# A hybrid layer on one core: attention pipelined over halves of the queries, packed diagonal maxima, sums by shuffle, and a projection spread over the last half and the FFN

## The reference

```python
x = x + attn_a(layernorm(x))   # 16 heads of 16, rotary embedding, causal softmax, projection Wo
x = x + ffn(layernorm(x))      # silu(x @ Wg) * (x @ Wu) @ Wd, hidden 768, int weights / 127
x = x + attn_b(layernorm(x))   # RWKV-like: token shift, low-rank mixes, decayed scan, group norm, gate, Wo
x = x + ffn(layernorm(x))      # the same FFN
```

```python
scores = einsum('bhtd,bhsd->bhts', q, k) / 4
scores = where(causal, -inf, scores)
out = einsum('bhts,bhsd->bhtd', softmax(scores), v)   # then out @ Wo.T
```

## Time and profile before

| | |
|---|---|
| median of 3 runs | 3501.13 us (3500.01 to 3502.6) |
| the profiled execution | 3503.35 us, its span 3501.6 |
| PE busy | 3000.5 us, 86% of the span |
| DVE busy | 2487.5 us, 71% |
| ACT busy | 1311.2 us, 37% |
| POOL busy | 1307.0 us, 37% |
| mean granted TensorE clock | 0.939 |

### The profile page before, as it was taken

One profiled execution on the slowest core, in us unless ns is written; L12 is line 12 of the kernel. 1 busy time (PEld: TensorE's weight loads), 2 busy tenths in 40 slices (PEclk: granted clock), 3 DMA queues, 4 the chain that ended last, 5 costly groups with the idle time before them and its releaser, 6 DMA issues.

```text
span 3501.6 us, 47094 instructions
## 1 busy us (share of the span) xinstructions
PE 3000.5 (86%) x17056; PEld 1850.4 (53%) x17056; DVE 2487.5 (71%) x5137; ACT 1311.2 (37%) x2721; POOL 1307.0 (37%) x1244
## 2 busy tenths in 40 slices
PE   2488989889889888889888898898988889898898
PEld 1236565365743567345763457635565355653667
DVE  4675787667775677856878568775687757876565
ACT  0264223622336322453225531265313643236322
POOL 0023551235512454124631347213462235522455
PEclk9699999999999999899998999899998999999999
DMA  3600032000510006000150002400023000330000
GB/s 130 110 2 13 19 64 54 2 13 19 79 39 13 2 19 98 20 14 10 29 97 2 14 10 46 80 2 13 19 46 71 2 13 19 52 66 2 1 1 13
DMA packets 68885, 115.01 MB, mean 33 GB/s; under 512 B 10795, under 2 KB 64075, under 8 KB 65531
## 3 DMA queue, kind: packets, MB, share of 16 engines
q1 hardware_dynamic: 68627, 111.51, 16.2%
HBM read 74.69 MB, written 33.65 MB: 31 GB/s over the span
## 4 chain that ended last, share of the span: by engine, by line
PE 46%; DVE 32%; POOL 9%; issue 5%; ACT 4%; DMA 2%; SPq 0%; DVEq 0%; ACTq 0%; POOLq 0%
DVE mxp L967 9%; PE PB L1311 7%; PE PB L1296 5%; PE PB L1386 5%; PE PB L1371 5%; PE PB L1282 4%; DVE arena L1156 4%; PE PB L1425 3%; PE PB L1344 3%; DVE arena L1165 2%; PE PB L1460 2%; DVE attn L890 2%; ACT arena L722 2%; PE PB L1450 2%; DVE stats L879 1%
## 5 line engine op out<-in xcount | busy, mean ns | idle before, releaser
L967 DVE TENSOR_REDUCE mxp<-PB 128x1 f32<-128x512 f32 (+3 forms) x1536 | 752.9, 549 | 160.8 <-PE PB L1282 87.1
L722 ACT ACTIVATE arena<-PB 128x512 f32<-128x512 f32 (+3 forms) x1536 | 650.5, 508 | 455.5 <-PE PB L1296 450.6
L1282 PE MATMUL PB<-arena 96*128 96x512 bf16 (+3 forms) x1536 | 513.0, 362 | 106.7 <-DVE mxp L967 64.3
L582 POOL TENSOR_SCALAR_AFFINE_SELECT arena<-arena 128x512 f32<-128x512 f32 x256 | 163.5, 639 | 1003.7 <-ACT arena L722 1003.3
L1296 PE MATMUL PB<-arena 99*128 99x512 bf16 (+3 forms) x1536 | 467.7, 344 | 26.5 <-DMA arena<-augT 19.3
L1282 PEld LDWEIGHTS PB<-arena 96*128 96x128 bf16 x1536 | 154.8, 102 | 428.0 <-DVE mxp L967 326.1
L1311 PE MATMUL PB<-arena 128*32 128x512 f32 (+3 forms) x3072 | 339.9, 515 | 15.5 <-ACT attn L711 13.7
L1371 PE MATMUL PB<-xh,wgu 128*128 128x512 f32 x768 | 313.7, 408 | 42.3 <-DVE xl L1034 29.0
L592 POOL TENSOR_TENSOR hl<-arena,hh 128x512 fp32r<-128x512 f32 x192 | 248.3, 1293 | 262.3 <-ACT hh L747 256.9
L1371 PE MATMUL PB<-xl,wgu 128*128 128x512 f32 x768 | 309.6, 403 | 2.8 <-issue 2.8
L1555 PE MATMUL PB<-arena 128*128 128x128 f32 x1792 | 235.4, 283 | 56.1 <-DVE arena L1156 46.7
(11 more groups left out here) (139 smaller groups left out, 5372.6 us busy)
## 6 DMA issues: line engine op xcount, KB each, us to landing
arena<-parts SPq DMA_DIRECT2D x112, 256.0 KB, 9.7
parts<-arena SPq DMA_DIRECT2D x192, 128.0 KB
arena<-parts SPq DMA_DIRECT2D x16, 768.0 KB, 18.4
arena<-in_x SPq DMA_DIRECT2D x16, 512.0 KB, 4.5
arena<-parts SPq DMA_DIRECT2D x16, 512.0 KB, 21.0
xres<-in_x SPq DMA_DIRECT2D x16, 512.0 KB, 4.8
out<-xres SPq DMA_DIRECT2D x16, 512.0 KB, 3.4
wgu<-arena SPq DMA_DIRECT2D x2, 768.0 KB, 4.5
```

The costliest lines, as they stand in the source:

```text
L582: pool.affine_select(out=a, in_=a, compare_op=ALU.is_ge, fill=0.0, base=0, pattern=[[0, HG], [1, 128]], channel_multiplier=-1).then_inc(ma ...
L722: act.activation(pt[:, U % 3, h, 0:n], bank(b, "score", t)[:, 0:n], ACT.Exp, scale=DH ** -0.5).then_inc(act_emptied, 1)
L967: dve.reduce_max(mxp[:, g % 2, h, col:col + 1], bank(b, "max", g * NPC + k)[:, 0:n], axis=AX.X).then_inc(dve_emptied, 1)
L1282: last = mm(ps[:, 0:n], qst[0:AUG, h, 128 * i:128 * i + 128], kst[0:AUG, h, s0:s0 + n], start=True, stop=not diag)
```

## The change

Attention is now planned in blocks of a group and a half of its queries (k = 2g + f, eight blocks).

- Units come half by half: four for half 0, then eight for half 1. Blocks of maxima alternate between 11 items (half 0) and 27 (half 1); `score_steps` works out how many scores each step has: none before 15 steps (LAG) after block 0's last maximum, then at most 0.6 a step, and 1.27 a step from 15 steps after block 1. After the last maximum each step has one unit of four scores.
- Maxima over 256 keys are packed two heads to a bank and one reduce, those over 128 keys four heads to a bank and one reduce; 152 items a sequence instead of 192.
- The join of the maxima stays on VectorE; the split into three parts moves to GpSimd (`max_parts`), per half and with five instructions. One DMA per half carries the three rows.
- ScalarE copies a half out when that half is done. `den` is a stream shuffle that puts the sum's row on all 32 partitions of a head, and a reciprocal over all 512 columns; `over_sums` follows per half.
- The projection items 0 and 1 stand after the scores of unit 44 of 48, items 2 and 3 after the first gate and up items of the FFN, with the residual and LayerNorm of half 1 inside the FFN. The transposes of half 1 move from the third to the fifth step of the first FFN.
- The first FFN uses the space of queries and keys (`ffn_sets`), the next sequence's x0 and the split buffers have other places, queries and keys are laid out half by half.

The core of the diff:

```diff
 def score_units():
-    return [(j, f) for j in range(NT) for f in (0, 1) if 128 * j < HALF * (f + 1)]
+    return [(j, f) for f in (0, 1) for j in range(4 * f + 4)]
 def max_pieces():
     out = []
-    for i in range(NT):
-        out.append((i, 0, min(HALF, 128 * (i + 1)), i))
-        if i >= 4:
-            out.append((i, HALF, 128 * (i + 1) - HALF, NT + i - 4))
+    for f in (0, 1):
+        if f:
+            out.append([((h,), i, 0, HALF, i) for i in range(4, NT) for h in range(HG)])
+        else:
+            out.append([])
+        for a in (3, 2, 1, 0):
+            n = 128 * (a + 1)
+            heads = [(h,) for h in range(HG)] if a >= 2 else [(0, 1), (2, 3)] if a else [tuple(range(HG))]
+            out[f] += [(hs, 4 * f + a, HALF * f, n, 4 * f + a + 4 * f) for hs in heads]
     return out
...
+def score_steps():
+    done, credit, out = 0, 0.0, []
+    for t in range(NMAX):
+        ready = [k for k in range(2 * NG - 1) if t >= BLOCK_END[k] + LAG]
+        most = HG * (LAST_UNIT[ready[-1]] + 1) if ready else 0
+        credit = min(credit + (1.27 if t >= BLOCK_END[1] + LAG else 0.6), 2.0)
+        n = max(0, min(int(credit), most - done))
+        credit -= n
+        done += n
+        out.append(done)
+    while done < NSC:
+        done = min(NSC, HG * (done // HG + 1))
+        out.append(done)
+    return out
...
+AUG_STEP = [min(BLOCK_END[k] + AUG_AT, NMAX + 1) for k in range(2 * NG)]
+UNIT_STEP = [step_of(HG * U + HG - 1) for U in range(NG * len(UNITS))]
+OUT_AFTER = [LAST_UNIT[k] + (3 if k < 2 * NG - 2 else 2) for k in range(2 * NG)]
+DEN_STEP = [UNIT_STEP[OUT_AFTER[k]] + 4 for k in range(2 * NG - 2)]
+O_STEP = UNIT_STEP[NG * len(UNITS) - 4]
...
+                    for t in range(STEPS):
+                        if t in BLOCK_END:
+                            max_parts(BLOCK_END.index(t))
+                        for U in DIAG_UNITS:
+                            if UNIT_STEP[U] == t:
+                                mask_unit(U)
+                        if t in DEN_STEP:
+                            over_sums(DEN_STEP.index(t))
+                        if t == O_STEP:
+                            over_sums(2 * NG - 2)
                     ln_scale(1, b, 0)
-                    ln_scale(1, b, 1)
+                    over_sums(2 * NG - 1)
...
+                    def den(k):
+                        g, f = k // 2, k % 2
+                        sums = sumT[:, f, :].rearrange("p (i t) -> p i t", i=4)
+                        dve.wait_ge(pv_copied, 8 * b + k + 1)
+                        if b or k >= 2:
+                            dve.wait_ge(attn_normed, 8 * b + k - 1)
+                        dve.stream_shuffle(sums, attn[:, 4 * f:4 * f + 4, g, :], [DH] * 32).then_inc(den_chain, 1)
+                        dve.wait_ge(den_chain, 16 * b + 2 * k + 1)
+                        dve.reciprocal(sums, sums).then_inc(den_chain, 1)
...
+                    den(2 * NG - 2)
...
+                    dve.wait_ge(x_loaded[0], 16 * (b + 1))
+                    residual("o", 0, 0)
+                    residual("o", 1, 0)
+                    ln_half(1, 0)
+                    den(2 * NG - 1)
+                    x_low(1, 0, (0, 1))
...
+                        if t == O_STEP:
+                            out_proj(0)
+                            out_proj(1)
+                    pv(NG * len(UNITS) - 2)
+                    pv(NG * len(UNITS) - 1)
+                    transpose_x(1, (0, 1))
...
+                            if e == 1 and k == 1:
+                                out_proj(2)
+                                out_proj(3)
```

The three parts of `max_parts`, five instructions in a chain:

```diff
+                        pool.tensor_scalar(parts_[0], m, -1.0, 1.0, ALU.mult, ALU.mult).then_inc(aug_chain, 1)
+                        pool.tensor_tensor(augf[:, :, :], m, parts_[0], ALU.add).then_inc(aug_chain, 1)
+                        pool.tensor_scalar(parts_[1], augf[:, :, :], -1.0, 1.0, ALU.mult, ALU.mult).then_inc(aug_chain, 1)
+                        pool.tensor_tensor(augf[:, :, :], augf[:, :, :], parts_[1], ALU.add).then_inc(aug_chain, 1)
+                        pool.tensor_scalar(parts_[2], augf[:, :, :], -1.0, 1.0, ALU.mult, ALU.mult).then_inc(aug_chain, 1)
```

More of the change, by code:

```diff
@@ L106, in ahead @@
                 add(nxt, kind, ns, who)
-        for t in range(NSC + DELAY):
-            if t < NSC:
+        for t in range(STEPS):
+            if t < NMAX:
                 add(b, "max", (t,), "dve")
@@ L112, in psum_plan @@
                 add(b, "v", (2 + V_AT.index(t),), "act")
[L113 to L117, removed]
+            if t in AUG_STEP:
+                add(b, "aug", (AUG_STEP.index(t),), "dve")
+            add(b, "score", scores_of(t), "act")
+            if t == O_STEP:
+                add(b, "o", (0, 1), "dve")
         add(b, "ln1", (0, 1), "dve")
-        add(b, "o", (3,), "dve")
         ffn(b, 1)
@@ L487, in split_tile @@
         def split_tile(e, s):
-            return halves(spl[e // 4][:, e % len(parts_out[e // 4]), s, :])
+            return halves(spl[e // 4][e % len(parts_out[e // 4])][:, s, :])
         def halves(a):
@@ L596, in _ @@
                         h_low_part(1, 0, e)
-                        if e == 1 and ahead:
+                        if e == 0:
+                            ln_scale(1, b, 1)
+                        if e == 5 and ahead:
                             ln_scale(0, b + 1, 0)
@@ L1070, in ffn @@
                             gate(k, s, e)
-                            if e == 4 and k == 1 and ahead:
+                            if e == 6 and k == 1 and ahead:
                                 x0_norm(b + 1, 0)
@@ L1313, in pv, with out_proj @@
                         last.then_inc(pv_units, 1)
-                    for t in range(NSC + DELAY):
-                        if t in (0, 2 * NPC):
-                            pe.wait_ge(stacked[t // (2 * NPC)], 9 * 16 * (b + 1))
-                        if t < NSC:
-                            max_item(t // NPC, t % NPC)
+                    def out_proj(n):
+                        wait_bank(pe, b, "o", n)
+                        pe.wait_ge(attn_normed, 8 * b + 2 * NG - 1 + n // 2)
+                        for a in (0, 1):
+                            for g in range(NG):
+                                last = mm(bank(b, "o", n)[:, D * a:D * a + D], attn[:, 2 * n + a, g, :], wo[:, g, :],
+                                          start=(g == 0), stop=(g == NG - 1))
+                        last.then_inc(filled, 1)
```

355 lines of the change are left out of this document (168 added, 187 removed).

## The result

The changed kernel takes 3659.58 us (median of 4 runs, 3642.74 to 3666.68) against 3501.86 for the kernel before in the same comparison (3500.01 to 3503.1): a ratio of 1.0445, 95% interval 1.0428 to 1.0462. It is 158 us slower, where 3488 was forecast and 3565 was the end of the range. The profiled execution took 3642.74 us, its span 3640.9, the fastest of the four; five of the sequences behind the first take 440.1 to 440.7 us of it.

The account below looks back on a forecast made before the run. VectorE and TensorE, blocking each other through the six-bank ring, were taken as the bound. 33.5+86+33+6+56.6=215.1 us against 216.9, 1.8 less a sequence, 14.4 over eight, off 3503.35, gave 3488 us; range 3400 to 3565.

Parts of the forecast that it names:

- The reciprocal: Denominators on VectorE: 512 columns taken at 3.0 us, ends 0.68 and 4.5; with the shuffle 3.7 us a half.
- the floor of the aggregates: Reciprocal estimate: 6-element aggregates start 0.07 us apart; taken off the 16-element reciprocal's 0.14, this gives 2.5 us for 512.
- Rival (a): Denominators: reciprocal cheap at 0.68 us, TensorE becomes the bound, 10.3 us a sequence less, 3406 us; chance 0.20.
- (b): Denominators: reciprocal costs 4.4 us, the floor hidden; 9.5 us a sequence more, 3564 us; chance 0.17.
- I take 90%: Steps 52 to 151: VectorE's busy share rises from 82% to 90%; ends 95% (81 us) and 82% (96 us).
- The third stretch: Steps 52 to 151, maxima and scores together: VectorE's 79.5 us over 0.90, less 2, gives 86 us.
- the stops of 2.5 us: Steps 52 to 151: TensorE and ScalarE stop some 2.5 us behind each 3.7 us denominator piece on VectorE.
- rival (c): Steps 12 to 51 and ahead of the FFN: TensorE at half clock, 5 us a sequence net, 3528 us; chance 0.13.
- Until the last product: Scores alone 23.5 us, half the projection 7.2, its wait for GpSimd 2.3: 33 us.
- Until the FFN: From last product to FFN: copy, shuffle, reciprocal, two x_low and waits on VectorE, 6 us against 18.5 before.
- steps 0 to 51: Ramp, VectorE-bound: 32.5 us of maxima, join, copies and V items plus 1 us for half clock, 33.5 us.
- Packing and the split: Maxima on VectorE: packing saves 2.5 to 6 us a sequence, 4 taken; moving the split to GpSimd saves 4.

Follow-up runs that it names:

- e5: e3 with the four denominator steps of halves 0 to 4 put behind four successive maxima, no piece over 0.7 us; 3456.61 us, ratio 0.9887.
- e1: The changed kernel with the 512-column reciprocal of halves 0 to 4 cut into four of 128 columns behind successive maxima; 3570.09 us, ratio 1.0204.
- e11: The changed kernel with the reciprocal over 256 of the 512 columns, that part of the softmax left out; 3555.38 us, ratio 1.0157.
- e6: e5 with all four projection items back behind the last value product, residual and LayerNorm of both halves ahead of the FFN; 3359.21 us, ratio 0.9606.
- e7: e3 with the split of the maxima, five small instructions per half, moved from GpSimd back to VectorE; 3554.82 us, ratio 1.0166.
- e10: e5 with GpSimd's scaling of half 6 put ahead of the mask of unit 44 instead of behind it; 3413.52 us, ratio 0.9753.
- e8: e3 with banks still packed but one reduce per head, 40 more instructions a sequence; 3521.3 us, ratio 1.0073.
- e9: e6 with the changed kernel's denominators, a shuffle and one reciprocal of 512 columns; 3536.24 us, ratio 1.0108.
- e3: The changed kernel with the denominators of before (transpose, reciprocal of 16, copy, transpose) per half in one piece of 2.0 us; 3484.57 us, ratio 0.9956.

## Why the prediction was wrong

**The reciprocal.** Taken at 3.0 us with ends 0.68 and 4.5, it is 3.353. By form, in e5, e1 and e11:

```profile
L1065 DVE RECIPROCAL recip<-sumT 128x16 f32<-128x16 f32 x64 | 15.3, 240 | 0.8
```

```profile
L1060 DVE RECIPROCAL sumT<-sumT 128x128 f32<-128x128 f32 x256 | 230.6, 924 | 0.8
```

```profile
L1056 DVE RECIPROCAL sumT<-sumT 128x256 f32<-128x256 f32 x64 | 112.2, 1753 | 2.2
```

From 256 to 512 columns it is 1.600 us, 6.25 ns a column, on 0.15 us. By this slope the 0.14 us between two starts at 16 columns were 0.10 for the columns and 0.04 for the rest: the floor of the aggregates, 0.07, was the wrong one to take off. By the prediction's own slope (6.8 us a sequence for each us) this is 2.4 us, 19 us in all: it turns 3488 into 3507 and no more. Rival (a) is refuted and (b) had the right sign with too high a price of the instruction (4.4) and too low a price of each us.

**The step that failed: "I take 90%".** The third stretch was reckoned as VectorE's work over a share, 79.5/0.90, less 2. The work was right. The share was 79%, under the lower end of 82% and near the 80% that the prediction named as a sign of being wrong, since I took the stops of 2.5 us (five, 12.5 us; measured 13.75) as something that VectorE's busy time already pays for. It doesn't, because TensorE is the second bound: its modelled busy time is 78.2 us of the 80.8 in e6. A stretch in which two engines need 79 and 78 us has no room for 14 us in which only one of them works, and none to make up time at half clock. I had priced the clock in the ramp and at the FFN (rival (c), 5 us a sequence, where its own terms give 4), where the row that I had read showed it, and not behind the stops that I forecast myself.

TensorE's busy and idle time of steps 52 to 151 show what stood in its place:

| us | length | TensorE busy | TensorE idle | VectorE busy | clock |
|---|---|---|---|---|---|
| e5 | 80.0 | 77.4 | 2.6 | 69.2 | 1.00 |
| e1 | 92.5 | 84.1 | 8.4 | 78.3 | 0.93 |
| after | 100.9 | 86.6 | 14.3 | 79.3 | 0.88 |

From e5 to the changed kernel the stretch grows by 20.9 us: 11.7 are idle time of TensorE, 9.2 are longer busy time for the same matmuls, since TensorE spent 22 us of it at 0.50. Of the 20.9 us, 8.4 are due to the length of the piece (e1 to after). The other 12.5 stand in e1 too, where the same work comes in short pieces: VectorE's share was 85% there and 86% in e7, so 90% was too high for this much work however it is cut. Adding the five stops to TensorE's need (78+13.75, 92 us) would have come nearer than the share, but misses what the clock takes, and it doesn't explain e1.

**Until the last product.** Forecast 33, measured 35.4: the base of 23.5 us (its terms add up to 23.1; e6: 23.9) and the projection's 7.2 (e10: 7.17) were right, the wait for GpSimd was 3.58 instead of 2.3, and the projection took 8.64 instead of 7.2 behind it. **Until the FFN** 7.6 instead of 6: the reciprocal's 0.35, and 1.6 us in which the last shuffle stood behind the normalization of half 0 (1635.23 above), which the prediction had as done by then; **FFN** 56.3, forecast 56.6; **steps 0 to 51** 34.7, forecast 33.5.

**Packing and the split.** The packing is worth about what was said (e8), and a chain of the split costs VectorE 1.1 us where 1 was taken (e7).

**What I read as a gain of 12.5 us behind the last product** (18.5 to 6) was to be paid back by 9.5 in the scores and 8.7 in the FFN in my own sum, so spreading the projection was forecast as a loss of 5.7 us a sequence, 46 in all. It cost 97 us in all beside fast denominators (e6 against e5) and 118 to 123 beside slow ones (e9 against the changed kernel). The mechanism was in the text, at less than half its size.

Of e1's 12.5 us over e5, 5.8 are idle and 6.7 busy time of TensorE. How much of the idle time the lower clock brought on itself was not measured: no run held the clock while TensorE waited. What makes the clock fall behind one stop and not behind another stays open too.

## What to carry to other kernels

Where two engines both fill a stretch and meet in a ring of buffers, don't divide the work of one by a share that looks reachable. Add the stops of the other to its own need as a first bound, and expect more: here 9.1 us of extra work in short pieces made the stretch 12.5 us longer. Before an instruction is stretched from a compact form to a wide one, price it per column: here three cheap passes around 16 columns (2.0 us) beat one over 512 (4.1 us), and cut into pieces between the producer's items they cost less still (e5 against e3). In this kernel, work that waits for a long chain did best behind other ready work of the same engine, as the projection of half 1 behind that of half 0; spread out, each part met its own wait.

## What the runs showed of the hardware

- VectorE's reciprocal: 0.240, 0.924, 1.753 and 3.353 us for 16, 128, 256 and 512 columns, where a copy of 512 took 0.41 us and a transpose 0.69. The Trainium skill ("VectorE: DVE Perf Modes", "First, the fixed hardware budget") gives a repeat count of 8. By it the prediction estimated 4.3 us for 512 columns; measured are 3.353, and the measurement decides.
- A stop of TensorE of 3.2 us was followed by 6.8 us at 1.2 GHz although TensorE was busy from the stop's end on; the stops of 0.68 to 1.57 us in e3's steps with both lowered nothing. The length of a single stop doesn't tell: behind the 1.83 us of the changed kernel the clock stayed at 1.00, and in e1 it was at 0.50 for over 6 us twice, behind stops of 0.6 to 0.8 us that followed one another closely.
- A stream shuffle of 128x512 takes 0.724 us from SBUF and 0.729 from PSUM (mean of 64 each): at this shape the source makes hardly a difference.
